# The low part of the gated product, made by GpSimd in the first fourteen steps

## What is computed

```python
def ffn(x, w_gate, w_up, w_down):          # hidden size 2048
    gate = einsum('bsd,hd->bsh', x, w_gate)
    up = einsum('bsd,hd->bsh', x, w_up)
    return einsum('bsh,dh->bsd', silu(gate) * up, w_down)

x = x + 0.5 * ffn(layernorm(x), w_gate, w_up, w_down)
x = x + attention(layernorm(x), w_qkv, w_out, q_gain)
x = x + 0.5 * ffn(layernorm(x), w_gate, w_up, w_down)
```

## Time and profile before

| | |
|---|---|
| median of 3 runs | 2738.82 us (2738.73 to 2738.93) |
| the profiled execution, its own time | 2739.15 us |
| its span | 2737.3 us |
| PE busy | 2689.7 us, 98% |
| DVE busy | 1787.4 us, 65% |
| ACT busy | 1180.1 us, 43% |
| POOL busy | 528.4 us, 19% |
| L965 on DVE, all 512 steps | 219.6 us, 429 ns each |

### The profile page before, as it was taken

One profiled execution on the slowest core, in us unless ns is written; L12 is line 12 of the kernel. 1 busy time (PEld: TensorE's weight loads), 2 busy tenths in 40 slices (PEclk: granted clock), 3 DMA queues, 4 the chain that ended last, 5 costly groups with the idle time before them and its releaser, 6 DMA issues.

```text
span 2737.3 us, 55236 instructions
## 1 busy us (share of the span) xinstructions
PE 2689.7 (98%) x22208; PEld 1957.6 (72%) x22208; DVE 1787.4 (65%) x5152; ACT 1180.1 (43%) x2197; POOL 528.4 (19%) x820
## 2 busy tenths in 40 slices
PE   7999999999999999999999999999999999999999
PEld 6677766776777776777767777777777766776776
DVE  8866676667666665656656666675756766676643
ACT  6454544454344443444434444334343544353422
POOL 0012212222131302112030220302113131313100
PEclk9999999999999999999999999999999999999999
DMA  5100000000000000000000000000000000000000
GB/s 202 62 19 7 19 7 3 7 19 22 1 9 17 24 1 3 22 1 24 2 5 21 11 15 1 7 18 21 5 17 9 17 9 2 9 17 17 2 9 16
DMA packets 51407, 47.71 MB, mean 17 GB/s; under 512 B 36304, under 2 KB 36304, under 8 KB 50640
## 3 DMA queue, kind: packets, MB, share of 16 engines
q1 hardware_dynamic: 51152, 44.19, 5.1%
HBM read 26.35 MB, written 9.44 MB: 13 GB/s over the span
## 4 chain that ended last, share of the span: by engine, by line
PE 88%; DVE 7%; issue 2%; ACT 2%; POOL 0%; DMA 0%; DVEq 0%; ACTq 0%; POOLq 0%
PE psum L1127 26%; PE psum L1129 26%; PE psum L1128 26%; PE psum L1287 2%; PE psum L1263 2%; PE psum L1299 2%; PE psum L1150 1%; DVE arena L959 1%; DVE arena L961 1%; ACT arena L844 1%; PE psum L1300 1%; DVE arena L954 1%; PE psum L1245 1%; DVE ss L888 1%; DVE arena L1038 1%
## 5 line engine op out<-in xcount | busy, mean ns | idle before, releaser
L1127 PE MATMUL psum<-arena,WU 128*128 128x256 f16 x2048 | 558.3, 273 | 1.5 <-DVE WU L900 1.5
L1127 PE MATMUL psum<-arena,WG 128*128 128x256 f16 x2048 | 558.2, 273 | 1.5 <-DVE arena L954 1.5
L1129 PE MATMUL psum<-arena,WG 128*128 128x256 f16 x2048 | 558.1, 273 | 0.0
L1129 PE MATMUL psum<-arena,WU 128*128 128x256 f16 x2048 | 558.0, 272 | 0.0
L1128 PE MATMUL psum<-arena,WG 128*128 128x256 f16 x2048 | 558.0, 272 | 0.0
L1128 PE MATMUL psum<-arena,WU 128*128 128x256 f16 x2048 | 557.9, 272 | 0.0
L959 DVE SCALAR_TENSOR_TENSOR arena<-arena,psum 128x256 f32<-128x256 f32 x512 | 215.0, 420 | 424.8 <-ACT arena L844 422.2
L844 ACT ACTIVATE arena<-psum,tscale 128x256 f32<-128x256 f32 x512 | 242.1, 473 | 563.6 <-PE psum L1129 562.6
L1127 PE MATMUL psum<-WD,arena 128*128 128x512 f16 x1024 | 388.9, 380 | 5.9 <-DVE WD L1088 4.3
L1129 PE MATMUL psum<-WD,arena 128*128 128x512 f16 x1024 | 388.4, 379 | 0.0
L1128 PE MATMUL psum<-WD,arena 128*128 128x512 f16 x1024 | 388.4, 379 | 0.0
(11 more groups left out here) (147 smaller groups left out, 4359.3 us busy)
## 6 DMA issues: line engine op xcount, KB each, us to landing
arena<-in_L_attn_x SPq DMA_DIRECT2D x16, 512.0 KB, 3.7
arena<-arena SPq DMA_DIRECT2D x128, 64.0 KB, 2.1
out<-arena SPq DMA_DIRECT2D x16, 512.0 KB, 2.8
WD<-in_L_ffn_w_up SPq DMA_DIRECT2D x4, 1024.0 KB, 6.3
arena<-in_L_ffn_w_down SPq DMA_DIRECT2D x4, 1024.0 KB, 8.5
WD<-in_L_ffn_w_gate SPq DMA_DIRECT2D x3, 1024.0 KB, 7.1
arena<-in_L_attn_w_qkv SPq DMA_DIRECT2D x1, 3072.0 KB, 10.2
WD<-in_L_ffn_w_gate SPq DMA_DIRECT2D x2, 512.0 KB, 4.2
```

The costliest lines, as they stand in the source:

```text
L1127: T_.matmul(o, lhs(0), rhs(0), start=first, stop=False)
L1129: return T_.matmul(o, lhs(1), rhs(0), start=False, stop=last)
```

## The change

In the steps 0 to 13 the subtraction that writes the low part is issued by GpSimd. From step 14 on DVE issues it as before. Operands, semaphore and place in the list of stages are the same.

```diff
+    POOL_STEPS = 14
+
...
+            def parts(j):
+                if j < POOL_STEPS:
+                    pool.wait_ge(s["h_hi"], j + 1)
+                    nc.gpsimd.tensor_tensor(H2(j)[1], fH[j % 2], H2(j)[0], ALU.subtract).then_inc(s["h_lo"], 1)
+
-            run({"stats": stats, "qk out": qkv_out, "unit": rotate, "exp": exp, "wd scales": wd_scales, "maxima sent": maxima_sent})
+            run({"parts": parts, "stats": stats, "qk out": qkv_out, "unit": rotate, "exp": exp, "wd scales": wd_scales, "maxima sent": maxima_sent})
...
             def parts(j):
+                if j < POOL_STEPS:
+                    return
                 dve.wait_ge(s["h_hi"], j + 1)
                 V_.tensor_tensor(H2(j)[1], fH[j % 2], H2(j)[0], ALU.subtract).then_inc(s["h_lo"], 1)
```

## The result

| | before | after |
|---|---|---|
| median, 22 runs each | 2739.06 us (2738.26 to 2740.14) | 2742.81 us (2741.09 to 2744.24) |
| the profiled execution, its own time | 2739.15 us | 2742.96 us |
| its span | 2737.3 us | 2741.2 us |
| POOL busy | 528.4 us | 537.5 us |

The ratio is 1.0014, with a 95% interval of 1.0007 to 1.0020: 3.75 us more, a small loss. The forecast was 2743.8.

A forecast was written before the change was run, and what follows sets the result against it. The DVE and ACT cycle sets the pace until 67.5 us, then PE. From 2739.15, -1.4 + 7.7 - 1.3 = +5.0 gives 2744.2, less 0.33 for the median: 2743.8 us, range 2739.5 to 2747.5.

The forecast's parts named there:

- The cycle: DVE and ACT rounds of about 8 us until 67.5 us: four subtractions of 0.34 us leave the path, -1.4 us.
- The cost on GpSimd: GpSimd's slower subtraction, 0.74 us against 0.43 on DVE, is hidden by more than 3 us per step; nothing added.
- "held up" rival: GpSimd's subtractions hold up DVE or ACT in each step, about +4 us on top of the forecast; chance 0.03.
- The place of the switch: POOL's change to the all-reduce cannot start before the last of the fourteen subtractions, ending about 87.5 us on the old clock.
- "hidden" rival: POOL's switch ahead of the all-reduce costs nothing or passes before its wait; 2736.4 to 2737.4 us, chance 0.03.
- The length L: Length of POOL's switch ahead of the all-reduce, taken as 10.7 us; delays the all-reduce's first reader by 7.7; chance 0.55.
- starved rival: POOL's switch ahead of the all-reduce takes 12.9 us under the DMA stream; 2746.0 to 2747.2 us with low clock, chance 0.14.
- short-switch rival: POOL's switch ahead of the all-reduce takes 5.74 us whatever the DMA does; 2740.1 us, chance 0.21.
- The 6 us of load: Skill's load price at POOL's switch, none given under traffic; would make the delay about 3 us, the sum below +1.6.
- What comes back: POOL's switch back to the power starts behind the stream, so PE's waits after its restart go; -1.3 us.
- The low clock: PE may stay longer at 1.2 GHz after its longer stop; 0 to 1.2 us in the range, none in the sum.

The follow-up runs named there:

- b_quiet: Kernel before, with w_qkv and w_out DMAs sent only after the first power behind the all-reduce and DVE's maxima of those weights placed later; 2738.67 us, ratio 0.9997.
- b_later_dma: Kernel before, with the DMAs of w_qkv and w_out sent only after the first power behind the all-reduce; 2741.68 us, ratio 1.0008.
- n12: Changed kernel, but GpSimd makes the low part in steps 0 to 11 only and DVE keeps 12 and 13; 2738.42 us, ratio 0.9998 to before.
- late_dma: Changed kernel, but the DMAs of w_qkv and w_out are sent only when the all-reduce is done; 2739.61 us, ratio 1.0001 to before.
- only13: Changed kernel, but GpSimd makes the low part of step 13 alone and DVE all others; 2744.59 us, ratio 1.0021 to before.
- b_warm: Kernel before, with 16 matmuls whose result nothing reads ahead of the first down product, in TensorE's stop; 2739.82 us, ratio 1.0002.
- b_warm_quiet: Kernel before with both b_quiet's later DMAs and maxima and the 16 unread matmuls in TensorE's stop, DVE making every low part; 2737.22 us, ratio 0.9993.
- n13_warm: Changed kernel, but GpSimd makes low parts in steps 0 to 12 only, plus 16 unread matmuls in TensorE's stop; 2738.37 us, ratio 0.9997 to before.

## Why the prediction held, and where its terms were off

**The cycle, -1.4.** Right: PE reached the weight turn 1.36 us earlier, and the kernel pairs with and without the subtractions differ by 1.6 to 1.8 us, of which 0.64 in the second pair came with the clock.

**The cost on GpSimd, none.** Right. A subtraction took 0.67 us (0.74 was taken), ended by ACT's L857 each time; no tanh waited for it. The "held up" rival is out.

**The place of the switch.** Right, and the core of the matter: the last subtraction was to end at 87.5 - 1.4 = 86.1 and ended at 86.01, and "issue" stood ahead of the all-reduce. The "hidden" rival is out here; with one step less it is what happens.

**The length L.** Taken as 10.7, measured 9.96, so this term was 0.7 us too large: L882 came 6.8 us late on the old clock (5.44 + 1.36), not 7.7. The starved rival's 12.9 is out, and the step that failed in it is the assumption that both switches are equal work. Quiet, one takes 5.7 to 6.2 us and the other 6.7 to 7.45. The forward switch lay wholly in the stream (1.02 DMA share in 94 to 96 us) and took 9.96 us for work of 5.8, a rate of 0.58, not 0.32. With this, the old switch back (7.3 us in the stream, then free) would be work of 4.2 + 3.4 = 7.6, near the 6.7 to 7.45 that it takes when quiet; in the kernel with late loads the same sum gives a rate near 0.7, so it is rough. The short-switch rival had one thing right, that the two differ by nature, though by about 1 us of the 4.9; the stream makes the rest. So 10.7 came close by luck: the row that I took it from was the longer switch with some 7 us of stream over it, the one to be forecast was the shorter with stream over all of it, and the two differences nearly cancel.

**The 6 us of load.** The Trainium skill ("GPSIMD Engine Reference", 2.1 Instruction dispatch) says that the first call to a freshly loaded kernel pays about 6 us of load. Ahead of the all-reduce on quiet queues the runs agree, 5.74 to 6.20; in the stream they show 9.6 to 10.

**What comes back, -1.3.** Too small: 2.0. The power came 7.2 us behind the all-reduce, below the 9.4 named, and the waits went. I added up the waits that the timeline shows in brackets, 1.11 and 0.21. From start to start the same two places cost 1.27 and 0.37, and the transposition behind the stop took another 0.3.

**The low clock, 0 in the sum.** It cost 0.64 more than before, inside the range that it was given. That the longer stop was the reason is not shown: after the same first stop of 4.0 to 4.1 us six matmuls ran slow in the kernel before and in b_quiet, eleven in b_later_dma and twelve in n12; after 6.94 us six (late_dma), after 10.87 us nine and after 10.86 twelve (only13). So 0.64 may as well be chance. And the view was too simple: b_warm shows that the low clock cost nothing before, since the wait for the power absorbed it. This term and the one before it are one account: with the late power gone, the low clock counts in full, some 1.9 us for nine products, of which the 44 matmuls won back 1.4 in the median.

**The sum.** +5.0 forecast, +4.1 at step 16 and +3.75 in the median. Of the 0.9 between +5.0 and +4.1, -0.9 is the delay of L882, -0.7 the larger recovery and +0.64 the clock. Another 0.2 was won back behind 121 us, where PE has a few waits of about half a microsecond; they were not followed up. That the forecast missed by 1 us only is owed in part to luck: to the row taken for L, and to terms that err in both directions.

## What to carry to other kernels

An engine that changes between kinds of operation, as GpSimd does here, can pay for the change at the place in its queue where it happens. A preparation that had always passed unseen behind a long wait becomes the critical path when one cheap instruction is put behind that wait, so ask of the last instruction of the old kind when it ends and what is next. Put it where the next input is late anyway: one subtraction less took 5 us off the time. And stalls that lie one behind the other share one slack: in the kernel before, one of them taken away moved the median by +0.7 or -0.6 us, neither clear of the noise, both by -2.0 (b_warm, b_quiet, b_warm_quiet). For this last one the interval still holds 1, but none of its eleven runs reaches the fastest of the fifteen of the kernel before (2737.98 against 2738.43).

## What the runs showed of the hardware

- GpSimd's change from a tensor operation to the all-reduce: 5.74 to 6.20 us on quiet queues, 9.59, 9.59 and 9.96 us with the DMA share near 1.0. From the all-reduce to the power: 6.70 to 7.07 us on quiet queues (at most that, as the profile names the input; but the power started 0.53 to 0.90 us behind it), 7.21 to 7.45 just behind the stream, 9.96 to 11.38 with 7 to 9 us of it in the stream. I had not expected that the two differ when quiet.
- A 128x256 subtraction with a float16 result takes 0.67 us on GpSimd and 0.43 on DVE.
- TensorE was granted 0.50 after stops of 2.88 us (101.46 in n13_warm) to 10.87 us, and kept 1.00 through one of 2.21 us (102.26 in b_warm). How many 128x512 matmuls then ran at 0.43 us apart did not follow the length of the stop: six to twelve after 4.0 to 4.1 us, nine and twelve after 10.9 us.
